# Image 0's sampling indices and weights in two halves, and depthwise sums in PSUM, in a four-layer convolution network

## What is computed

```python
y = leaky_relu(bn(conv1x1(gn(x))))                   # 256 -> 256 channels
xp = inproj(y)                                       # what is sampled from
t = leaky_relu(bn(depthwise3x3(y)))
offset, mlog = off(t), mask(t)                       # 72 and 36 values per pixel
mask = softmax(mlog over the 9 points of each of 4 groups)
for each pixel, group g (4) and point k (9):         # grid sample of xp
    x0, y0 = floor(position(pixel, k) + offset)      # sampling index
    samp = 4 corners, weighted with wx, wy and mask  # sampling weights
dout = outproj(sum over the 9 points of samp)
... batch norm, squeeze-excite, fc1, leaky_relu, fc2, + y
```

## Time and profile before

| | |
|---|---|
| median of 3 runs | 7383.66 us (7372.89 to 7388.69) |
| the profiled execution | 7394.4 us, of which its span 7392.6 us |
| POOL, busy | 4743.2 us, 64% of the span |
| DVE, busy | 5174.9 us, 70% |
| PE, busy | 3808.3 us, 52% |
| ACT, busy | 1073.1 us, 15% |
| DMA | 129 GB/s mean |
| first gather starts, last gather starts | 188.91 us, 6364.79 us |
| phases A(1), A(2), A(3), F(0) | begin at 210, 758, 1293 and about 1780 us |

### The profile page before, as it was taken

One profiled execution on the slowest core, in us unless ns is written; L12 is line 12 of the kernel. 1 busy time (PEld: TensorE's weight loads), 2 busy tenths in 40 slices (PEclk: granted clock), 3 DMA queues, 4 the chain that ended last, 5 costly groups with the idle time before them and its releaser, 6 DMA issues.

```text
span 7392.6 us, 45558 instructions
## 1 busy us (share of the span) xinstructions
PE 3808.3 (52%) x10560; PEld 2000.5 (27%) x10560; DVE 5174.9 (70%) x5212; ACT 1073.1 (15%) x1619; POOL 4743.2 (64%) x4676
## 2 busy tenths in 40 slices
PE   7142241341574516533764346426656652497968
PEld 4121120220221204311322124213223431243533
DVE  5778787786777668856777679767777976432546
ACT  2110000100111002211100022111101210111334
POOL 0777777777777777777777777777777777300000
PEclk9576675675787758766887678767878876698979
DMA  3453543634433333364433333554333345310047
GB/s 104 146 149 99 184 133 113 201 111 153 137 123 124 102 103 114 123 221 159 128 118 114 104 112 123 186 181 136 123 113 106 123 152 190 99 37 34 34 168 185
DMA packets 547458, 954.04 MB, mean 129 GB/s; under 512 B 284448, under 2 KB 349984, under 8 KB 531616
## 3 DMA queue, kind: packets, MB, share of 16 engines
q0 software_dynamic: 221184, 604.27, 26.2%
q1 hardware_dynamic: 326176, 348.65, 14.6%
HBM read 792.21 MB, written 160.37 MB: 129 GB/s over the span
## 4 chain that ended last, share of the span: by engine, by line
POOL 50%; issue 22%; PE 12%; DVE 9%; DMA 3%; ACT 1%; SPq 1%; DVEq 0%; POOLq 0%; ACTq 0%
POOL ring L371 50%; PE PS L692 11%; DVE ring L1340 3%; DVE dbuf L1346 2%; DMA img<-d_dram 2%; ACT img L1061 1%; DMA ring<-table,idx_stage 1%; DVE sm L1750 0%; DVE stats L1860 0%; POOL idx_stage L387 0%; SPq L593 0%; DMA img<-q_dram 0%; PE PS L789 0%; DMA o_dram<-img 0%; ACT wb_sb L1061 0%
## 5 line engine op out<-in xcount | busy, mean ns | idle before, releaser
L371 POOL DMA_INDIRECT ring<-table,idx_stage x4608 | 4714.6, 1023 | 1434.9 <-issue 1371.4
L1340 DVE TENSOR_TENSOR ring<-ring,wt 128x576 f32<-128x576 f32 x2048 | 1414.2, 753 | 992.8 <-DMA ring<-table,idx_stage 868.5
L1346 DVE TENSOR_REDUCE dbuf<-ring 128x64 f32<-128x2304 f32 x512 | 2070.2, 4043 | 31.4 <-DMA d_dram<-dbuf 3.3
L692 PE MATMUL PS<-img,wb_sb 128*128 128x512 f32 (+1 forms) x3328 | 1635.2, 652 | 471.0 <-DVE img L1405 299.6
L692 PE MATMUL PS<-img,wa_sb 128*128 (+1 forms) x1984 | 930.1, 630 | 620.9 <-DVE img L1724 244.9
L692 PEld LDWEIGHTS PS<-img,wb_sb 128*128 128x128 f32 x3328 | 689.5, 211 | 1382.7 <-issue 1088.9
L692 PEld LDWEIGHTS PS<-img,wa_sb 128*128 128x128 f32 x1984 | 396.9, 202 | 1124.6 <-issue 1064.5
L692 PE MATMUL PS<-sm,params 128*128 128x4 f32 (+1 forms) x32 | 9.1, 354 | 825.5 <-DVE sm L1384 761.0
L692 PE MATMUL PS<-wa_sb,cb 128*128 128x108 f32 (+1 forms) x1024 | 237.0, 397 | 370.9 <-DVE cb L1405 370.9
L789 PE MATMUL PS<-params,img 128*128 128x128 f32 x256 | 62.9, 426 | 691.2 <-DMA img<-d_dram 691.2
L1061 ACT ACTIVATE img<-PS,sm 128x512 f32<-128x512 f32 x384 | 247.8, 680 | 1090.1 <-PE PS L692 1090.1
(11 more groups left out here) (194 smaller groups left out, 2973.4 us busy)
## 6 DMA issues: line engine op xcount, KB each, us to landing
ring<-table,idx_stage POOLq DMA_INDIRECT x4608
table<-cb SPq DMA_DIRECT2D x64, 512.0 KB, 6.0
img<-y_dram SPq DMA_DIRECT2D x64, 512.0 KB, 6.5
q_dram<-img SPq DMA_DIRECT2D x32, 1024.0 KB, 4.2
img<-q_dram SPq DMA_DIRECT2D x32, 1024.0 KB, 6.2
img<-in_x SPq DMA_DIRECT2D x8, 2048.0 KB, 12.2
y_dram<-cb SPq DMA_DIRECT2D x64, 256.0 KB, 2.3
d_dram<-dbuf SPq DMA_DIRECT2D x128, 128.0 KB
```

What stands on the lines that cost most here:

```text
L371: nc.gpsimd.indirect_dma_start(out=ring[:, g, p * CORNERS * GC:(p + 1) * CORNERS * GC], out_offset=None, in_=tab[b], in_offset=bass.Indire ...
L692: return nc.tensor.matmul(o, l, r, start=start, stop=stop, **kw)
L1340: last = vec.tensor_tensor(rg, rg, weights.unsqueeze(2).to_broadcast([P, n, GC]), ALU.mult)
L1346: vec.tensor_reduce(dbuf[:, j, g * GC:(g + 1) * GC], ring[:, g, :].rearrange("p (k c) -> p c k", c=GC), AX_X, ALU.add).then_inc(sem("ring_ ...
```

## The change

1. `HALF = TILES // 2`. For image 0 alone, indices and weights are made by `index(0)` for tiles 0 to 15 and `index(1)` for tiles 16 to 31, 576 values per partition each. `index(0)` stands behind the A2 turns 0 and 1 (four chunks), `index(1)` behind turn 3 and the rest of tile 0's units. `terms(b, half)` gives them slots in `img1` alone, behind `OM`, where `dwacc` was, so the depthwise of later turns can go on reading `img2`.
2. `dwacc` moves from `img1` to two banks of PSUM, for all four images.
3. POOL starts image 0 when the tables are stored and `idx_made` is 1, runs three quads of tiles, waits for `idx_loaded` and goes on.
4. In A(0) DVE takes tile 0 of image 0 around the last A2 turn and tile 1 within `index(1)`; SP stores both. ACT does its part of a half (`hats`) between its turns 1 and 2, and behind turn 3.
5. A(1) takes 11 tiles as before, A(2) 10 (one extra at the start, not two) and A(3) 9 (no extra at the start): 2 + 11 + 10 + 9 = 32.

The core of the diff:

```diff
-        dwacc = [img1[:, TILES * 3 * PTS + h * CHUNK:TILES * 3 * PTS + (h + 1) * CHUNK] for h in range(2)]
+        dwacc = [PS[:, 2 * h + 1, :] for h in range(2)]
...
-                pool.wait_ge(sem("idx_loaded"), 16 * (b + 1))
+                if b == 0:
+                    for h in range(2):
+                        pool.wait_ge(sem(f"t_stored{h}"), 16 * TAB_STORES * PAIRS + 16)
+                    pool.wait_ge(sem("idx_made"), 1)
+                else:
+                    pool.wait_ge(sem("idx_loaded"), 16 * (b + 1))
                 nc.gpsimd.tensor_copy(idx_stage[:, 0, :], idx[:, b % 2, 0:2 * PTS]).then_inc(sem("idx_staged"), 1)
-                with pool.Fori(0, TILES // 4 - 1) as i:
-                    quad(b, i, False)
+                first = 0
+                if b == 0:
+                    first = HALF // 4 - 1
+                    with pool.Fori(0, first) as i:
+                        quad(b, i, False)
+                    pool.wait_ge(sem("idx_loaded"), 16)
+                with pool.Fori(0, TILES // 4 - 1 - first) as i:
+                    quad(b, i + first, False)
...
                 if gi is not None:
-                    for _ in range(1 if b == B - 1 else 2):
+                    for _ in range(B - 1 - b):
                         stream.extra(gi, store_sums)
...
                 if b == 0:
+                    for _ in range(2):
+                        stream.extra(0, store_sums)
...
+                if b == 0:
+                    nc.scalar.preload_act_table(ACT.Identity)
+                    with act.Fori(0, PAIRS // 2) as i:
+                        a2(i)
+                    hats(0)
+                    for i in range(PAIRS // 2, PAIRS):
+                        a2(i)
+                    hats(1)
+                    barrier()
...
                     dve.wait_ge(sem("wt_loaded"), 16 * (gi + 1))
-                    stream.extra(gi)
+                    if b < B - 1:
+                        stream.extra(gi)
                 image_stats(b)
-                if gi is not None and b < B - 1:
+                if b == 1:
                     stream.extra(gi)
...
+                def index(half):
+
+                    t0, n = (half * HALF, HALF) if b == 0 else (0, TILES)
+                    t_, (top, scale) = terms(b, half)
+                    nth = count_of(b, half)
...
+                    if b:
+
+                        less_maximum()
+                    else:
+                        done(dve, "dE", (half + 1) * (CHUNKS // 2) - 1)
...
+                    made = idx[:, 0, part] if b == 0 else img1[:, 0:TILES * PTS].bitcast(U32)
+                    vec.tensor_tensor(tp(made), tp(t_[7]), v("g_base").unsqueeze(1).to_broadcast([P, n, PTS]), ALU.add)\
+                        .then_inc(sem("idx_made"), 1)
+                    if b == 0:
+                        if half == 1:
+                            dve.wait_ge(sem("idx_made"), 2)
+                            dve.sem_inc(sem("idx_loaded"), 16)
+                        less_maximum()
+                    if gi is not None or half == 1:
+                        stream.extra(gi or 0)
+                    dve.wait_ge(sem("mask_exp"), nth)
...
                 depthwise(0, False)
+                if b == 0:
+                    own.settle()
+                    with dve.Fori(0, PAIRS // 2) as i:
+                        own.enter(i, K2 - 1)
+                        a2(i)
+                    own.leave(PAIRS // 2)
+                    index(0)
+                    a2(PAIRS // 2)
+                    stream.unit(0, 0, 0, 0)
+                    a2(PAIRS // 2 + 1, True)
+                    for g in range(1, G):
+                        stream.unit(0, 0, g, 0)
+                    stream.taken[0] = 1
+                    index(1)
+                    barrier()
+                    dve.sem_inc(sem("wt_loaded"), 16)
+                    barrier()
+                    return
```

More of the change, by code:

```diff
@@ L72 @@
 OBUFS = 3
+HALF = TILES // 2
 PARTS = 4
@@ L207, in network_kernel, with count_of, terms @@
         assert used[0] <= 496, used[0]
+        def count_of(b, half):
+            return 1 + half if b == 0 else b + 2
+        def terms(b, half):
+            if b == 0:
+                n = HALF * PTS
+                slots = [img1[:, TILES * 3 * PTS + j * n:TILES * 3 * PTS + (j + 1) * n] for j in range(8)]
+                at = TILES * 3 * PTS + 8 * n
+                return slots, [img1[:, at + j * HALF * G:at + (j + 1) * HALF * G] for j in range(2)]
+            n = TILES * PTS
+            return [img1[:, 3456 + j * n:3456 + (j + 1) * n] for j in range(4)] \
+                + [img2[:, 4608 + j * n:4608 + (j + 1) * n] for j in range(4)], \
+                [cb[:, j * TILES * G:(j + 1) * TILES * G] for j in range(2)]
         coef = cb[:, 0:KC * K2 * K2]
@@ L1115, in a2, with hats @@
                             .then_inc(sem("dZ"), 1)
[L1116 to L1132, removed]
+                def hats(half):
+                    t_, _ = terms(b, half)
+                    nth = count_of(b, half)
+                    act.wait_ge(sem("dx_dy"), nth)
+                    A_(t_[2], t_[0], ACT.Abs, bias=neg_one)
+                    A_(t_[3], t_[1], ACT.Abs, bias=neg_one)
+                    A_(t_[0], t_[0], ACT.Abs)
+                    A_(t_[1], t_[1], ACT.Abs).then_inc(sem("act_own"), 1)
+                    act.wait_ge(sem("act_own"), nth)
+                    for j in (0, 1, 2, 3):
+                        last = A_(t_[j], t_[j], ACT.Relu, bias=one_c, scale=-1.0)
+                    last.then_inc(sem("hats"), 1)
+                    act.wait_ge(sem("logit_less"), nth)
+                    A_(t_[6], t_[6], ACT.Exp).then_inc(sem("mask_exp"), 1)
+                if b == 0:
[8 more added lines that the diff above has]
+                else:
+                    loop(ACT.Identity, a2)
+                    barrier()
+                    hats(1)
                 barrier()
@@ L1540, in A @@
-                link(last)
-                for t in (4, 5):
-                    last = vec.tensor_scalar(T(t), T(t), -MAGIC, None, ALU.add)
-                link(last)
-                for a, t in ((0, 4), (1, 5)):
-                    last = vec.tensor_tensor(T(a), T(a), T(t), ALU.subtract)
-                last.then_inc(sem("dx_dy"), 1)
-                link(vec.scalar_tensor_tensor(out=T(7), in0=T(5), scalar=float(W), in1=T(4), op0=ALU.mult, op1=ALU.add))
-                made = idx[:, 0, :] if b == 0 else img1[:, 0:TILES * PTS].bitcast(U32)
```

103 lines of the change are left out of this document (50 added, 53 removed).

## The result

The changed kernel takes **7343.5 us** (median of 5 runs, 7342.44 to 7349.42) against 7383.66 us (median of 5 by then, 7372.89 to 7388.69) before: a ratio of 0.9948, 95% interval 0.9933 to 0.9963. That is 40.2 us less; the forecast was 26.6 us less. Its profiled execution took 7342.44 us. That of before lay 10.7 us above its own median, so the two profiles differ by 52 us where the medians differ by 40; some 12 us of what the traces show are spread between executions.

What follows compares the result with a forecast made beforehand. POOL's 4608 gathers were taken to bound the kernel. Earlier start -30.1, contention +3.5, PSUM sums -20 and A(3) stall +20 sum to -26.6 us, from 7383.66 to 7357.0 us, range 7334 to 7380.

Steps and rivals of the forecast that it cites:

- The rule: Whole kernel: other engines count only by moving POOL's start, lengthening gathers or filling the ring; image 0's shift passes on fully.
- Term 1: A(0): index chain for half the tiles right behind turn 1 starts the first gather at 158.8, not 188.9; gain 30.1 us.
- Term 2: A(0): gathers lengthened by the second index half and two turns' leaky_relu; loss 3.5 us, bounds 1.7 to 4.6.
- Term 3: A(1) to A(3): with dwacc in PSUM, 99 gathers under the depthwise each lose 0.20 us less; gain 20 us.
- gathers at the edges: Depthwise of A(1) to A(3): if these gathers lose more than 0.20 us, the PSUM gain rises to 27 us.
- Term 4: Start of A(3): without its extra tile, POOL waits for a ring slot; loss 20 us, bounds 12 to 25.
- the PSUM sums bring relief: Depthwise: denies the rival that PSUM sums leave gathers as long, total -6.6 us, 7377; chance 0.12.
- the stall came: A(3) start: denies the rival that DVE reaches the ring sooner, no stall, total -46.6 us, 7337; chance 0.12.
- DVE did not hold POOL in A(0): Denies the rival that DVE's detour in A(0) frees first slots late, losing 15 us of head start, 7372; chance 0.10.
- that last rival: Depthwise: each instruction with its running sum in PSUM takes x us more, making the kernel slower; chance 0.08.
- x = 0.18: Depthwise: added us per instruction with its sum in PSUM at which the total is 0; at 0.75, +173 us, 7557.

Runs made afterwards that it cites:

- The start alone: Changed kernel with depthwise sums back in SBUF and one extra tile at the start of each of A(1), A(2), A(3): 7373.17 us, ratio 0.9964 to the kernel before.
- the even tiles: Changed kernel with one extra tile at the start of each of A(1), A(2) and A(3): 7328.90 us, ratio 0.9915 to the kernel before.
- the separate runs: The start alone, -27 us, and the kernel before with only the depthwise sums moved to PSUM: 7367.91 us, ratio 0.9955, -33 us.

## Why the prediction was right, and where its sum was off

**The rule.** That the time goes by POOL's gathers held: the shift of the gathers at the end of image 0, 49.0 us, reaches the end of the kernel, and the parts add up. The last gather starts at 6308 us where the forecast had 6338. The rule holds on a chip where POOL waits 50 us for DVE, and not where it waits 1300; the forecast named no such chip, and no row of the kernel before shows one.

**Term 1, the start.** 31.0 us for 30.1: the chain took 6.9 us and not 7.1, and turn 1 ended 0.7 us earlier. DVE's other work went in the order laid out. The first unit ended at 192.1 us (forecast 195), the bias adds of turn 3 at 200.5 (202), the fourth unit at 220.6 (222), and A(1) began at 270.7 (273). POOL had no wait for a slot in A(0) over 0.3 us.

**Term 2, contention in A(0).** Forecast +3.5. The start alone is 31.3 us ahead at tile 0, 31.5 at tile 12 and 30.9 at tile 32. So it was under 1 us, and the 1152 gathers of image 0 take 1204.2 us in all there, against 1205.0 before. The term was too large.

**Term 3, the sums.** This is the term that was mis-sized most: 20 us forecast, 33 us in the runs (interval 21 to 45), 36 us in the gathers. The mechanism was right, and so was the count (99 forecast, 96 found). The price was not: 0.20 us is what a gather loses in an unbroken depthwise, the row, and only 24 of the 96 are there. The other 72 begin where units break it into pieces, with more of the step left, and lose 0.30 us. The mean over the 96 is 1.223 - 0.946 = 0.277 us, 26.6 us in all. The remaining 8 us lie at leaky_relu, which the forecast left out: some 4.5 us because the gathers now begin later in it, 3.6 us by one gather held for 4.53 us, which is luck. The forecast's upper bound of 27, for "gathers at the edges", was the depthwise's own value; it did not reach to the neighbours.

**Term 4, the stall.** Right in place, number and size: after 24 tiles of gathers, 20.8 us over the issue time where 19.5 was worked out, with the 1.3 us of a second wait where 2 was allowed for. The slot was free at 1316.26 us, 35.2 us after A(3) began at 1281.06; the steps laid out in the forecast gave 34.6 (from 1293.4 to 1328.0). Measured against the even tiles, the net price is 17 us in the traces. A(2), where one tile stays, had no wait for a slot, as forecast.

**The sum.** With the measured terms: -31.0 + 0.4 - 36 + 22.1 = -44.5 us, where image 0 shows -49.0; by the separate runs -27 - 33 + 22 = -38, where the runs show -40.2. Both agree within the spread. The forecast's -26.6 was short by 13.6 us, nearly all of it term 3's: the result is in the range because the range was wide enough for that, not because each term was. The rivals fell: the PSUM sums bring relief, the stall came, DVE did not hold POOL in A(0), and the depthwise step is not longer (751 ns against 749). In that last rival the two points of the forecast were not summed alike: at x = 0.18 it takes off 26.6 us, at x = 0.75 only 6.6; with 26.6 the second is +153 us, not +173. Nothing else hangs on it.

## What to carry to other kernels

Where a chain of software-issued gathers sets the time, write down three things before a change: when the first can start, which instructions of other engines hold one while it is issued, and the longest stretch in which the consumer frees no slot, against what the ring covers. Price the second by the mean over all gathers that meet the instruction, edges and neighbours too, and not by a row in the middle of a long run: what a gather loses here is what is left of the instruction when it begins, less 0.13 us (0.946 - 0.82). And measure on a second chip before a gain of half a per cent is believed: here the change was worth -0.5% on one and +0.5% on another, where POOL waited for DVE for 1293 us in place of 76.

## What the runs showed of the hardware

- A gather (indirect DMA issued by POOL) is held by a depthwise step with both tensor inputs in SBUF, with its output in SBUF or in PSUM, and not by one with one input in PSUM: 1.22 to 1.23 against 0.946 us. It ends 0.82 us behind the end of the instruction under which it began (1139 of 1155 before), not behind the chain; four of 1155 were held to the end of a chain of multiplies, for up to 4.53 us. Nine gathers under a tensor_scalar from SBUF into SBUF took 1.07 to 1.17 us.
- A 512-value scalar_tensor_tensor that reads and writes its sum in PSUM takes 751 ns, against 749 in SBUF; a tensor_scalar from SBUF takes 743 ns into PSUM and 478 into SBUF.
- The kernel before took 7384 to 7404 us on some chips and 8592 and 8711 us on two others, at a granted clock of 0.71 in place of 0.75. In the traces of its variants there, 26 to 30% of the chain falls to releasers that the profile does not name; the cause is open.
